# A second semaphore for the rows of an attention output, and the store that waits on it

## What is computed

```
x = x + L0(gn(x))    # three gates from max/mean pools, 7x7 convolutions, a softmax over the three branches
x = x + L1(gn(x))    # 3x3 convolution 256 -> 256, weights mixed from block-circulant projections
x = x + L2(gn(x))    # channel excitation from the mean of a wavelet low band
x = x + L3(gn(x))    # shifted window attention, windows of 8x8, 8 heads, with a relative bias and a mask
```

## Time and profile before

| | us |
|---|---|
| median of 3 runs | 2878.24 |
| lowest, highest | 2876.93, 2885.32 |
| the profiled execution's own time | 2871.03 |
| its span, first to last instruction | 2869.2 |

### The profile page before, as it was taken

The page is one execution under the profiler, slowest core; times in us unless marked ns, Lnnn a source line. Parts: engine busy times, 40 slices in busy tenths (PEclk is TensorE's granted clock), DMA queues, the critical chain, the costliest instruction groups (busy, mean ns, idle before and its releaser), DMA issues. The chain is left out here.

```text
span 2869.2 us, 68252 instructions
## 1 busy us (share of the span) xinstructions
PE 2368.1 (83%) x27252; PEld 1337.8 (47%) x27252; DVE 2303.8 (80%) x4579; ACT 1654.8 (58%) x4200; POOL 1390.7 (48%) x1132
## 2 busy tenths in 40 slices
PE   0376828899798988899798988899798988899788
PEld 0232315444554545444554545444454545444555
DVE  7877866879888797979878797979878797978665
ACT  0322137754866568664866558664866558664665
POOL 2413561355724564355724565354824565354454
PEclk9968968999899989999899999999999999999999
DMA  5400310015010241004110241004110141001111
GB/s 147 121 1 16 122 42 24 31 38 170 16 46 23 82 133 31 31 31 148 45 46 24 76 139 32 31 31 139 55 46 24 62 145 39 31 30 45 61 52 47
DMA packets 90337, 176.13 MB, mean 61 GB/s; under 512 B 37526, under 2 KB 50470, under 8 KB 80422
## 3 DMA queue, kind: packets, MB, share of 16 engines
q1 hardware_dynamic: 90022, 171.77, 18.2%
HBM read 98.86 MB, written 72.86 MB: 60 GB/s over the span
## 5 line engine op out<-in xcount | busy, mean ns | idle before, releaser
L2021 PE MATMUL F<-g_raw,cw_hi 128*128 128x512 f16 x2304 | 700.0, 386 | 28.1 <-DVE ytj L1454 10.9
L879 POOL TENSOR_TENSOR xs<-xs,rec 128x512 f32<-128x512 f32 x256 | 282.0, 1102 | 731.4 <-DVE rec L1796 728.5
L1158 ACT ACTIVATE xs<-xs,mx 128x64 f32<-128x64 f32 x1792 | 447.4, 336 | 131.4 <-DVE mx L1791 131.4
L2021 PE MATMUL F<-g_raw,cw_lo 128*128 128x512 f16 x1152 | 443.6, 385 | 0.0
L2021 PEld LDWEIGHTS F<-g_raw,cw_hi 128*128 128x128 f16 x2304 | 222.6, 99 | 296.4 <-issue 19.6
L1780 DVE TENSOR_TENSOR xs<-SP,bias 128x512 f32<-128x512 f32 (+2 forms) x384 | 181.8, 501 | 120.2 <-PE SP L2112 118.8
L864 POOL TENSOR_TENSOR tmp<-X,uw 128x512 f32<-128x512 f32 x128 | 171.5, 1351 | 179.1 <-DVE X L1636 114.3
L1795 DVE TENSOR_REDUCE sums<-xs 128x8 f32<-128x512 f32 x256 | 172.9, 675 | 95.1 <-ACT xs L1158 69.2
L2080 PE MATMUL QP<-tok_hi,qkv_hi 128*128 128x512 f16 x470 | 182.8, 389 | 51.9 <-ACT qq L1139 28.9
L1369 DVE SCALAR_TENSOR_TENSOR g_raw<-l0c,gn,g_raw 128x512 f16<-128x512 f32 x192 | 171.2, 934 | 50.0 <-ACT g_raw L1016 35.2
L2140 PE MATMUL O<-prt,vv 64*32 64x64 f32 x8192 | 175.0, 228 | 32.1 <-ACT prt L1165 28.3
(11 more groups left out here) (322 smaller groups left out, 5786.7 us busy)
## 6 DMA issues: line engine op xcount, KB each, us to landing
scratch_x<-X SPq DMA_DIRECT2D x32, 1024.0 KB, 7.4
xs<-scratch_x SPq DMA_DIRECT2D x56, 512.0 KB, 3.6
out_x<-xs SPq DMA_DIRECT2D x56, 512.0 KB, 2.8
X<-in_x SPq DMA_DIRECT2D x25, 1024.0 KB, 5.5
l0c<-scratch_t SPq DMA_DIRECT2D x8, 1876.0 KB, 9.7
l0c<-in_x SPq DMA_DIRECT2D x7, 1024.0 KB, 5.6
l0c<-scratch_t SPq DMA_DIRECT2D x8, 640.0 KB, 12.3
l0c<-scratch_t SPq DMA_DIRECT2D x8, 576.0 KB, 13.9
```

The costliest lines, as they stand in the source:

```text
L879: G.tensor_tensor(keyed(sc[:, u % 4, :]), keyed(sc[:, u % 4, :]), rec[:, u % 4, :].unsqueeze(2).to_broadcast([P, 8, TOK]), ALU.mult).then_ ...
L1158: last = S.activation(keys, keys, ACT.Exp, bias=mx[:, u % 4, i:i + 1])
L2021: last = T.matmul(F[:, n % 2, :], wgt[:, ci, C3 * comp + dx, P * co:P * co + P], win[which], start=(ci == 0 and dx == 0 and j == 0), stop= ...
```

## The change

The clear of `sm`, the wait in front of it and the semaphore `x4_set` are taken out. The store of a row waits, through `wait_read`, for the count of `qp_taken` that belongs to the second channel tile of its row. Nothing is moved in the played orders.

```
-        x4_set = sem("x4_set")
...
                 def store_row(row):
-                    sp.wait_ge(x4_set, CT * (row + 1))
+                    wait_read(sp, f"p{CT - 1}.{row}")
...
                     last.then_inc(qp_taken, 1)
-                    wait_read(dve, f"p{co}.{r}")
-                    V.memset(sm[:, 3, :], 0.0).then_inc(x4_set, 1)
```

## The result

The changed kernel takes 2871.01 us in the median of 18 runs (2858.15 to 2876.91), the kernel before, beside it, 2879.67 us (2869.50 to 2885.32). The ratio is 0.9968 with a 95% interval of 0.9956 to 0.9979: 9.2 us faster, between 6.0 and 12.7. The forecast was 6.5 us, to 2871.7. That 0.32% is just past what a measurement of this kernel can tell from no change. The profiled execution's span fell from 2869.2 to 2860.6 us, 8.6 us.

What follows compares the result with a forecast made beforehand. VectorE was taken to bound the stages between convolutions, TensorE the convolution. Terms of 0.88 us an image gave 6.2 us for seven, plus 0.3 us in the last: 6.5 us, from 2878.2 to 2871.7 us, range 2862 to 2883.

Steps and rivals of the forecast that it cites:

- The bound: Per image: TensorE sets the convolution (135.1 of 139 us); time off VectorE counts between convolutions, little within one.
- The price on VectorE: After each addition with a ready follower, VectorE gains 0.13 to 0.20 us; 128 at 0.15 us are 19.2 us.
- Second normalisation: Two gains in front of the moments the normalisation starts from, taken in full: 0.34 us an image.
- Convolution: Additions within it get 0, covered by TensorE; two early ones share 0.13 us an image with two under the gates.
- Gates: Two additions under the gates, followers partly held by TensorE; with two early in the convolution, 0.13 us for all four.
- End of the convolution: Gains of 0.31 us, capped by line 1457's need of the last matmul, 0.13 us before it; 0.15 us taken.
- First normalisation and reduce steps: 0.13 us before line 1396 and 0.13 us before line 1474, each taken in full per image.
- Behind the eighth front: Last image's additions, mostly followed by waits for TensorE: 0.3 us in all, 0.1 us of it at the last store.
- The store: Row store's wait on SP: released up to 0.09 us sooner, hidden except at the kernel's very end.
- All of VectorE's time coming back: Rival: 128 x 0.15 us pass at all additions, 19.2 us faster, to 2859.0 us; chance 0.12.
- The next instruction gains no start: Rival: followers of additions held as long as now; only the store's 0.09 us is left, 2878.1 us; chance 0.20.
- The clock as a slower case: Rival: images 4 to 7 take a slower clock pattern in first normalisations, 8.8 us lost, 2887.0 us; chance 0.10.

Runs made afterwards that it cites:

- e2: Changed kernel plus a one-element clear behind each pair of additions, without wait or semaphore; ratio to the kernel before 0.9953.
- e3: Changed kernel plus VectorE's wait for its own additions, with no clear; ratio to the kernel before 0.9992.
- e4: Kernel before plus a second clear behind the first, waiting for the first clear's semaphore; ratio to the kernel before 1.0051.
- e11: Changed kernel with five waits in a row at each of six places between an image's excitation and the next one's gates; ratio to the kernel before 1.0011.
- e1: Kernel before with only the store's wait changed to qp_taken, wait and clear kept on VectorE; ratio to the kernel before 0.9993.
- e10: Changed kernel with one addition an image, in the convolution's middle, moved behind VectorE's next convolution step (line 1439); ratio to the kernel before 0.9981.

## Why the prediction held, and where its steps failed

The mechanism held: the wait was the price, the followers moved as forecast, and a part of VectorE's time passed. The total came out by luck in part: its single terms were wrong in both directions, and for the stages that can be measured 0.34 + 0.15 + 0.13 = 0.62 us an image was taken where 0.68 us came.

**The bound.** VectorE between the convolutions, TensorE within: half right. The windows of the changed kernel, by the same stages as the earlier trace rows:

```profile
1350.00:1386.00 36.00, 25.95 (x390) 16.19 (x388) 31.28 (x88) 21.49 (x49) 25.33 (x22) 0.86 0.38 124
1386.00:1427.00 41.00, 31.48 (x404) 20.15 (x402) 37.12 (x64) 39.12 (x122) 34.39 (x33) 0.92 0.08 27
1510.00:1535.00 25.00, 18.47 (x330) 11.02 (x330) 22.67 (x47) 17.74 (x47) 12.15 (x9) 1.00 0.14 44
1535.00:1674.00 139.00, 135.62 (x1188) 69.18 (x1186) 114.32 (x176) 76.16 (x186) 75.17 (x55) 0.99 0.23 76
```

TensorE's 135.1 of 139 us in the convolution before left 3.9 us of idle time, and that was the thing to look at: a stage that is 97% full can still be lengthened by a tenth of a us at the places where its idle time is.

**The price on VectorE.** Right: 0.13 to 0.20 us for an addition, 0.29 us at one place, 15.2 us in all against 19.2. The difference is mostly the followers that wait for others. That the clear itself is free and the wait is the price was right (e2, e3).

**The places.** This is the step that failed, and two errors nearly cancelled.
- Second normalisation, 0.34 us taken, 0.21 measured. I looked for idle time of VectorE and found none before 1533.40, so I took VectorE for the chain. The chain was TensorE's, which meets VectorE earlier. TensorE in the kernel before and then in the changed one:

```profile
1523.78 0.39 PE L2080 MATMUL QP<-tok_hi,qkv_hi 128*128 128x512 f16 x1 [0.67 <-DVE xs L1804]
```

```profile
1518.70 0.39 PE L2077 MATMUL QP<-tok_hi,qkv_hi 128*128 128x512 f16 x1 [0.47 <-DVE xs L1803]
```

 TensorE waits for the second addition itself. The first hold lies in front of that addition and passes in full: 0.67 - 0.47 = 0.20 us. The second lies behind it, after `qp_taken` has risen, and only delays moments that TensorE takes up late. e4 agrees: two places lengthened, +0.25 us on VectorE, +0.12 us of stage.
- Convolution, at most 0.13 us taken together with the gates, 0.43 measured. One place is in front of line 1361, early in it, 0.13 us. The other is in the middle. VectorE before, then changed:

```profile
1618.65 0.88 DVE L1804 SCALAR_TENSOR_TENSOR xs<-QP,wm,xs 128x480 f32<-128x480 f32 x2 [1.21 <-PE QP L2096]
1619.59 0.06 DVE L1808 MEMSET sm<- 128x2 f32 x1
1619.74 0.75 DVE L1440 SCALAR_TENSOR_TENSOR X<-F,gm,X 128x512 f32<-128x512 f32 x1
```

```profile
1613.45 0.88 DVE L1803 SCALAR_TENSOR_TENSOR xs<-QP,wm,xs 128x480 f32<-128x480 f32 x2 [1.22 <-PE QP L2093]
1614.24 0.74 DVE L1439 SCALAR_TENSOR_TENSOR X<-F,gm,X 128x512 f32<-128x512 f32 x1
```

 From the additions' end 0.21 us, now -0.09: line 1440 has waits of its own, the dearest case of a held clear. Behind it VectorE forms the inputs of the lower half's convolution. The starts of the convolution's 432 matmuls show both places as steps between the two traces: 0.13 us from 22.8 us after the first matmul on, 0.31 us more from 91.7 us on, and none elsewhere. 0.13 + 0.29 is the measured 0.43 within 0.01. e3 takes 0.18 of it back, as the wait without the clear costs 0.18 us less there, and e4 adds 2 x 0.13. "TensorE covers these" was wrong for two of four places.
- Gates: 0.06 us taken, 0.00 measured (27.66 us).
- End of the convolution: 0.15 us taken, which is more than the 0.13 us that its own row allowed. The cap was the right thought, and too lax: 0.04 us of it is left in the stage behind.
- First normalisation and reduce steps, 0.26 us taken. No length there is steady; by e11 somewhat under half of a large hold passes, so 0.3 to 0.5 us for six places. Not settled better than that.
- Number of places: 16 in each of seven fronts were taken, and 16 behind the eighth. The first addition comes at 471.9 us, between the second image's reduce steps and its gates: that front has only 12, without places 12 to 15, and 20 come behind the eighth.
- Behind the eighth front: 0.3 us taken. No run tests it; the length there scatters by 3.6 us between two traces of the changed kernel.

The sum by what was measured is 0.68 x 7 = 4.8 us, with the inferred 2 to 3 us some 7 to 8 us, against 9.2 (6.0 to 12.7) measured; the forecast of 6.5 us lies inside too. So half of the 9.2 us is shown place by place, and the rest is not. The forecast's sign of images of 323.3 us where they were 324.2 can't be read: the six distances between the additions at the end of the convolution are 324.0 to 327.8 us before and 322.7 to 325.1 after.

**The store.** Right: nothing by itself (e1).

**The rivals.** All of VectorE's time coming back (19 us) is outside the interval. "The next instruction gains no start" is refuted by every follower shown. The rule of the Trainium skill that was set beside it ("VectorE: DVE Perf Modes", section "The DRAIN you can't avoid", a semaphore after each operation costs nothing extra) doesn't hold here for a semaphore that the next instruction waits for: with such a wait and no clear followers start 0.034 us after the additions' end, without it 0.081 us before. The clock as a slower case didn't come, though such falls are real: three in e4's trace, one in e10's. That more hold brings more of them is not shown.

## What to carry to other kernels

An instruction whose only work is to raise a second semaphore after a wait for its own engine costs the wait, not its duration: here 0.12 us where its follower is simple, 0.20 to 0.29 us where the follower has several waits of its own. To price a hold, ask for each place who waits for what stands behind it: a hold in front of an instruction that another engine waits for passes in full, one behind that instruction's release passed nothing here, even with no idle time of the engine for 10 us; and an engine that is 97% busy in a stage doesn't cover its neighbours at the places where its last 3% lie. Where the total scatters, measure the distance between two fixed instructions in each repetition: here it showed steps of 0.04 us where two executions of one program differ by 13 us.

## What the runs showed of the hardware

- The same program had spans of 2860.6 and 2873.8 us in two profiled executions, with mean granted clocks of 0.937 and 0.928. A stretch at the lower clock costs 1.2 us in a convolution (140.40 and 140.05 us for 139.23 and 138.80) and 2.4 to 3.9 us in the second normalisation (e4, e10), where TensorE's matmuls are on the path between waits. I had expected 2.2 us an image at most, as one case among rivals, not in every run.
- A short clear that isn't held takes 7 ns of its neighbours' time, though its row says 60 ns (e2).
- VectorE's followers start 0.08 us before the end of the work ahead, also behind an instruction of only 0.24 us, the shorter of the two that make an addition. A wait for that work puts them 0.034 us behind its end (e3).
